# Selective attention on one core: each score row split into the larger and the smaller of its two halves before the largest values are picked

## The chip, the cores and the metric

The kernel runs on one core of one Trainium2 chip. The metric is the device time in microseconds (us) of one execution of the whole program. The engines named here are PE (TensorE, matrix products), DVE (VectorE), ACT (ScalarE), POOL (GpSimd) and SP (SyncE, which issues transfers). They run side by side and wait for each other on semaphores.

## The reference, cut to what matters

The program is a chain of four blocks over 4 sequences of 512 tokens with 128 channels. The change lies in the attention of the third block: 16 heads of 8 channels, and for every query only the largest scores take part.

```python
NHEAD = 16
FACTOR = 5
U = min(L, int(FACTOR * math.log(L)) if L > 1 else L)      # 31 for L = 512
scores = jnp.einsum('bhqd,bhkd->bhqk', Q, K) / math.sqrt(D)
thresh = jax.lax.top_k(scores, U)[0][..., -1:]
scores = jnp.where(scores < thresh, -jnp.inf, scores)
attn = jax.nn.softmax(scores, axis=-1)
context = jnp.einsum('bhqk,bhkd->bhqd', attn, V)
```

So for each of 4 x 16 x 512 score rows of 512 values the 31st largest must be found, and smaller ones drop out of the softmax.

## The kernel before, in words

`full_attention` serves two attentions of the program: this one (`top` is true) and a smaller one in the fourth block, with 8 heads and no selection. The work is cut into tiles of 128 queries by 512 keys of one head, one score row to a partition. Four heads make a quad, two neighbouring tiles of a quad a pair. The selective attention has 64 quads and 128 pairs; `p` counts pairs.

Each engine has a program of its own, written out as a loop over `p`, and the semaphores set the order. For a pair:

- PE multiplies queries and keys of a quad (`score`, L1636), and ACT copies the products from PSUM to one of eight score buffers in SBUF (`copy_scores`, L1723), three pairs ahead.
- DVE finds the largest values (`pick`). MAX8 (L1786) writes the eight largest of a row in order; the replacement (L1788), which runs as MATCH_VALUE_LOAD and MATCH_REPLACE8, copies the row with these eight overwritten by a very low value. Four rounds of MAX8 with three replacements between them give 32 values in order. The two rows of a pair take turns, so that each instruction waits for the last but one. At the end DVE waits for all picks and writes the negated and scaled maximum of both rows (TENSOR_SCALAR of 2 columns, L1792).
- ACT waits for the negated maximum and takes the exponential (`exponential`, L1707).
- POOL waits for it too. For each of the two rows it compares the scores with the 31st largest (TENSOR_SCALAR, L1812, output `kept`) and multiplies the exponentials by the result (TENSOR_TENSOR, L1815).
- PE transposes the products (`turn`, L1645), ACT copies them (L1714), PE multiplies by the values (`weigh`, L1655).

Every four quads, that is every eight pairs, a step is finished: DVE takes a reciprocal (`invert`, L1760), three pairs later multiplies by it (`normalise`, L1766), and two pairs after that adds a bias (`finish`, L1771). In DVE's loop these stand ahead of `pick` of their pair:

```python
for p in range(LAST):
    if (s := step_at(p, 3)) is not None:
        invert(s)
    if (s := step_at(p, 6)) is not None:
        normalise(s)
    if (s := step_at(p, 8)) is not None:
        finish(s)
    if p < 2 * Q:
        pick(p)
```

Elsewhere in the program, `add_product` adds a gated result to the residual: POOL multiplies four slices (L242) and DVE adds each when it is there (L248). A stage of the second block multiplies by decays on DVE (L1382) and on POOL (L1411), and an earlier line of that stage multiplies on DVE (L1364) while POOL clears a buffer (MEMSET, L1400).

Of the kernel before, what the change touches and what calls it, by code (L numbers as in the profile page):

```python
# [17 lines left out]
P = 128  # L18
# [232 lines left out]
class Memory:  # L251


    def __init__(self, nc, ctx):
        self.nc = nc
        self.slabs = ctx.enter_context(nc.sbuf_tensor("slabs", [P, NSLAB * TOK], F32))
        where, width = offsets(CONST_PARTS)
        self.const = ctx.enter_context(nc.sbuf_tensor("constants", [P, width], F32))
        self.psum = ctx.enter_context(nc.psum_tensor("psum", [P, 8, 512], F32))
        self.masks = ctx.enter_context(nc.sbuf_tensor("window_masks", [P, 320], F32))[:, :]  # L260
        self.weights = ctx.enter_context(nc.sbuf_tensor("weights", [P, 5632], F32))

        def constant(name, rows=P):
            at, n = where[name]
            return self.const[0:rows, at:at + n]

        self.mean, self.ident = constant("mean"), constant("ident")
        self.centre, self.mean_halves = constant("centre"), constant("mean_halves")
        self.tiny, self.ones_row = constant("tiny"), constant("ones_row", 1)
# [1251 lines left out]
A_PARTS = [("q2", 4 * P), ("k2", 4 * P), ("v2", P), ("o2", 4 * P), ("v_row2", P), ("bq2", 4), ("bk2", 4), ("bo2", 1), ("pick2", 4)]  # L1521


def attention_plan(selective):


    if selective:
        quads = [[(b, t, 4 * c + i, i) for i in range(4)] for b in range(BATCH) for t in range(4) for c in range(4)]
    else:
        quads = []  # L1530
        for b in range(BATCH):
            quads += [[(b, 0, i, i) for i in range(4)], [(b, 0, 4 + i, i) for i in range(4)], [(b, 1, i, i) for i in range(4)],
                      [(b, 2, 0, 0), (b, 2, 1, 1), (b, 3, 0, 2)]]
    return quads


def full_attention(nc, m, xn, out, w, heads, scale, top, key_slab, query_slab, mask=None):
# [6 lines left out]
    dh, groups = P // heads, heads // 4  # L1544
    width = dh + 1
    quads = attention_plan(top)
    Q, STEPS, passes = len(quads), len(quads) // 4, 7 if top else 1
    present = sum(len(quad) for quad in quads[0:4])
    keys = m.slab(key_slab, groups).rearrange("p (g t) -> p g t", g=groups)
    q = m.slab(query_slab, groups).rearrange("p (g t) -> p g t", g=groups)  # L1550
# [1 line left out]
    scores = [m.slab(13 + n // 4)[:, 512 * (n % 4):512 * (n % 4) + 512] for n in range(8)]  # L1552
    probs = [m.slab(15)[:, 512 * n:512 * n + 512] for n in range(4)]
    probsT = [m.slab(16 + n // 4)[:, 512 * (n % 4):512 * (n % 4) + 512].rearrange("p (k q) -> p k q", k=4) for n in range(8)]
    work = [m.slab(18)[:, 512 * n:512 * n + 512] for n in range(2)]
    kept = [m.slab(18)[:, 1024 + 512 * n:1536 + 512 * n] for n in range(2)]
    ctx = m.slab(19)[:, 0:512].rearrange("p (c q) -> p c q", c=4)
    normed = m.slab(19)[:, 512:1024].rearrange("p (c q) -> p c q", c=4)
# [56 lines left out]

    with phase(nc, "score_product scores_copied picked0 picked1 picked2 picked3 negmax_ready exp_done kept_ready probs_ready "
                   "pT_product pT_copied pv_done ctx_copied den_product inverted expanded spread_product normed_ready "
                   "out_product out_done") as (
            block, score_product, scores_copied, picked0, picked1, picked2, picked3, negmax_ready, exp_done, kept_ready, probs_ready,
            pT_product, pT_copied, pv_done, ctx_copied, den_product, inverted, expanded, spread_product, normed_ready,  # L1620
            out_product, out_done):
        finished = probs_ready if top else exp_done
        LAST = 2 * Q + 12

# [126 lines left out]
        @block.vector  # L1751
        def _(dve):
            picked = [picked0, picked1, picked2, picked3]
            taken = [0, 0, 0, 0]

            def invert(s):
                dve.wait_ge(den_product, s + 1)
                if s >= 1:
                    dve.wait_ge(expanded, s)
                nc.vector.reciprocal(inverse, ps[:, 7, 0:present]).then_inc(inverted, 1)  # L1760

            def normalise(s):
                dve.wait_ge(spread_product, s + 1)
                if s >= 1:
                    dve.wait_ge(out_product, s)
                nc.vector.tensor_tensor(normed, ctx, ps[:, 7, :].rearrange("p (c q) -> p c q", c=4), ALU.mult).then_inc(normed_ready, 1)  # L1766

            def finish(s):
                dve.wait_ge(out_product, s + 1)
                if top:  # L1770
                    nc.vector.tensor_scalar(out[:, s * P:s * P + P], ps[:, 7, 0:P], w["bo"], None, ALU.add).then_inc(out_done, 1)  # L1771
                else:
                    nc.vector.scalar_tensor_tensor(out=out[:, cols(s)], in0=ps[:, 7, :], scalar=w["bo"], in1=mask,
                                                   op0=ALU.add, op1=ALU.mult).then_inc(out_done, 1)

            def pick(p):
                own = pair(p)
                b, slot = quads[own[0][0]][0][0], 4 * (own[0][0] % 2) + own[0][1]
                dve.wait_ge(scores_copied, number(*own[-1]) + 1)
                for k in range(passes):  # L1780
                    for side in range(len(own)):
                        eight = tops[:, slot + side, 8 * (k // 2):8 * (k // 2) + 8]
                        if k:
                            dve.wait_ge(picked[b], taken[b] - len(own) + 1)
                        if k % 2 == 0:
                            nc.vector.max(eight, work[side] if k else scores[slot + side]).then_inc(picked[b], 1)  # L1786
                        else:
                            nc.vector.match_replace(out=work[side], in_to_replace=eight, in_values=scores[slot + side] if k == 1 else work[side],  # L1788
                                                    imm_value=MASKED).then_inc(picked[b], 1)
                        taken[b] += 1  # L1790
                dve.wait_ge(picked[b], taken[b])
                nc.vector.tensor_scalar(tops[:, slot:slot + len(own), 32], tops[:, slot:slot + len(own), 0], -scale, None,  # L1792
                                        ALU.mult).then_inc(negmax_ready, 1)

            for p in range(LAST):
                if (s := step_at(p, 3)) is not None:
# [3 lines that stand above are left out]
                if (s := step_at(p, 8)) is not None:  # L1800
                    finish(s)
                if p < 2 * Q:
                    pick(p)

        if top:
            @block.gpsimd
            def _(pool):
                for p in range(2 * Q):
                    for g, j in pair(p):
                        n, slot = number(g, j), 4 * (g % 2) + j  # L1810
                        pool.wait_ge(negmax_ready, p + 1)
                        nc.gpsimd.tensor_scalar(kept[n % 2], scores[slot], tops[:, slot, TOPK - 1:TOPK], None, ALU.is_ge).then_inc(kept_ready, 1)  # L1812
                        pool.wait_ge(kept_ready, n + 1)
                        pool.wait_ge(exp_done, n + 1)
                        nc.gpsimd.tensor_tensor(probs[j], probs[j], kept[n % 2], ALU.mult).then_inc(probs_ready, 1)  # L1815
# [827 lines left out]
```

## Time and profile before

| | us |
|---|---|
| median of 3 runs | 5038.49 |
| the three runs | 5038.49, 5037.72, 5050.88 |
| span of the profiled execution | 5048.7 |
| DVE busy in it | 3273.2 |
| PE busy | 3797.4 |
| ACT busy | 2549.2 |
| POOL busy | 2087.9 |

The span runs from the first to the last instruction of the profiled execution; the list of runs doesn't mark which of the three it is. Busy times are sums over stages that have different limits, so the stage of the change is looked at by itself. An instruction's recorded time reaches from its start to its end, and on DVE the next may start before that end; what an instruction costs its engine is the distance from its start to the next start.

### The profile page before, as it was taken

Reading aid. Unit: us, or ns where it says so; the run is one execution under the profiler, and the core shown is the slowest. Engines: PE = TensorE matmul, PEld = TensorE weight load, DVE = VectorE, ACT = ScalarE, POOL = GpSimd, SP = SyncE. Lnnn points to the kernel's source line nnn. Section 1 sums busy time; section 2 is a strip of 40 time slices with the busy share of each in tenths; the row PEclk is TensorE's granted clock in tenths of the full one; section 3 lists DMA queues with packets and bytes.
Section 4 is the critical chain, followed back from the end, with each engine's and each line's share of the span. In section 5 each row is a group of like instructions: output and inputs, shape, how many; then the busy total and the mean of one; then the engine's idle time right before and its main releaser. Section 6 shows DMA issues by size and latency. Waiting matters only on the chain. (4 is left out here: it accounts for less than half of the span.)

```text
span 5048.7 us, 81560 instructions
## 1 busy us (share of the span) xinstructions
PE 3797.4 (75%) x28548; PEld 2346.0 (46%) x28548; DVE 3273.2 (65%) x6732; ACT 2549.2 (50%) x7024; POOL 2087.9 (41%) x1599
## 2 busy tenths in 40 slices
PE   5288788788789788797778659766666666587897
PEld 2156466466466465564253533333333333355664
DVE  5777476476575575674352643599999999832344
ACT  2199498498597695794121211233333333335443
POOL 0177276375474573671222200266666666500000
PEclk8599899899899899998586878755555555567998
DMA  0011111111111111111000000000000000000000
GB/s 18 28 43 47 36 47 46 36 49 47 36 46 52 30 47 51 34 47 48 0 1 9 1 26 0 0 1 1 1 1 1 1 1 1 1 7 11 12 1 9
DMA packets 48662, 110.09 MB, mean 22 GB/s; under 512 B 8944, under 2 KB 9200, under 8 KB 46704
## 3 DMA queue, kind: packets, MB, share of 16 engines
q1 hardware_dynamic: 48240, 104.66, 6.7%
q8 instruction: 241, 3.95, 0.3%
q14 instruction: 181, 1.48, 0.1%
HBM read 31.23 MB, written 1.05 MB: 6 GB/s over the span
## 5 line engine op out<-in xcount | busy, mean ns | idle before, releaser
L1089 POOL TENSOR_TENSOR slabs<-slabs 128x512 f32<-128x512 f32 x768 | 953.2, 1274 | 379.7 <-DVE slabs L956 322.5
L1786 DVE MAX8 slabs<-slabs 128x8 f32<-128x512 f32 x1084 | 695.1, 686 | 58.3 <-ACT slabs L1723 58.3
L1812 POOL TENSOR_SCALAR slabs<-slabs 128x512 f32<-128x512 f32 x256 | 400.2, 1563 | 470.4 <-DVE slabs L1792 470.4
L1707 ACT ACTIVATE slabs<-slabs 128x512 f32<-128x512 f32 x316 | 212.1, 721 | 727.5 <-DVE slabs L1792 727.5
L859 ACT ACTIVATE slabs<-slabs 128x96 f32<-128x96 f32 x1536 | 556.5, 366 | 19.2 <-PE psum L670 13.3
L1645 PE MATMUL psum<-constants,slabs 128*128 128x128 f32 x1264 | 306.3, 407 | 299.2 <-POOL slabs L1815 298.9
L1788 DVE MATCH_REPLACE8 slabs<-slabs 128x512 f32<-128x512 f32 x768 | 515.5, 683 | 0.0
L623 PE MATMUL psum<-slabs 128*128 128x512 f32 x768 | 411.7, 663 | 128.5 <-DVE slabs L956 63.0
L1078 POOL TENSOR_TENSOR slabs<-slabs 128x768 f32<-128x768 f32 x192 | 282.3, 1470 | 499.1 <-DVE slabs L931 499.1
L1636 PE MATMUL psum<-slabs 8*128 8x512 f32 (+1 forms) x632 | 346.2, 1086 | 164.4 <-ACT slabs L1723 164.1
L1645 PEld LDWEIGHTS psum<-constants,slabs 128*128 128x128 f32 x1264 | 223.3, 209 | 383.4 <-POOL slabs L1815 343.3
L941 DVE TENSOR_REDUCE slabs<-slabs 128x16 f32<-128x1024 f32 x192 | 234.2, 1220 | 225.2 <-ACT slabs L810 225.2
L670 PE MATMUL psum<-constants,slabs 128*96 128x128 f32 x1536 | 245.0, 283 | 153.8 <-ACT slabs L852 151.2
L1815 POOL TENSOR_TENSOR slabs<-slabs 128x512 f32<-128x512 f32 x256 | 325.2, 1270 | 21.4
L623 PEld LDWEIGHTS psum<-slabs 128*128 128x128 f32 x768 | 151.4, 210 | 353.7 <-issue 186.2
L242 POOL TENSOR_TENSOR slabs<-slabs 128x512 f32<-128x512 f32 x12 | 17.5, 1486 | 665.9 <-POOLq L63 665.9
L859 ACT ACTIVATION_READ_ACCUMULATOR slabs<-slabs 128x1 f32 x1536 | 292.3, 190 | 0.0
L810 ACT ACTIVATE slabs<-psum 128x1024 f32<-128x1024 f32 x192 | 196.7, 1025 | 140.9 <-PE psum L623 131.4
L964 DVE TENSOR_TENSOR slabs<-slabs 128x512 f32<-128x512 f32 x384 | 248.7, 688 | 28.2 <-POOL slabs L1089 28.0
L1636 PEld LDWEIGHTS psum<-slabs 8*128 8x128 f32 (+1 forms) x632 | 112.6, 293 | 301.4 <-ACT slabs L1723 282.2
L852 ACT ACTIVATE slabs<-psum 96x512 f32<-96x512 f32 x384 | 222.5, 579 | 43.1 <-PE psum L670 42.9
L670 PEld LDWEIGHTS psum<-constants,slabs 128*96 128x96 f32 x1536 | 155.1, 128 | 190.5 <-issue 173.7
(389 smaller groups left out, 7979.6 us busy)
## 6 DMA issues: line engine op xcount, KB each, us to landing
slabs<-slabs SPq DMA_DIRECT2D x192, 192.0 KB, 2.5
slabs<-slabs SPq DMA_DIRECT2D x192, 128.0 KB, 2.5
slabs<-F1A SPq DMA_DIRECT2D x7, 2176.0 KB, 8.4
slabs<-slabs SPq DMA_DIRECT2D x144, 64.0 KB, 2.1
slabs<-F1F SPq DMA_DIRECT2D x6, 580.5 KB, 4.9
slabs<-S SPq DMA_DIRECT2D x4, 645.0 KB, 5.8
weights<-M SPq DMA_DIRECT2D x1, 2184.0 KB, 9.4
weights<-R SPq DMA_DIRECT2D x2, 1079.5 KB, 5.1
```

The source lines that it names most:

```text
L623: last = nc.tensor.matmul(ps[:, i, :], tokens, w(name, 512 * half, 512), start=True, stop=True)
L670: last = nc.tensor.transpose(ps[0:KEYS, 7, n * P:n * P + P], probs[:, 4 * part + n, :], m.ident)
L859: last = nc.scalar.activation(probs[:, n, :], masked[:, n, :], ACT.Exp, bias=shifts[:, n:n + 1], accum_out=denom[:, n:n + 1])
L964: nc.vector.tensor_tensor(roped[:, at, :].rearrange("p h (s i) -> p h s i", s=2), cosines[:, at, :].rearrange("p h (s i) -> p h s i", s=2) ...
L1078: nc.gpsimd.tensor_tensor(probs, probs, scale, ALU.mult).then_inc(probs_ready, 1)
L1089: nc.gpsimd.tensor_tensor(out[:, at, :], normed[u % 2][:, at, :], table, ALU.mult).then_inc(rope_done, 1)
L1636: nc.tensor.matmul(ps[:, j, :], q[rows, h // 4, b * SEQ + t * P:b * SEQ + t * P + P], keys[rows, h // 4, cols(b)], start=True, stop=True). ...
L1645: last = nc.tensor.transpose(ps[:, 4 + n % 2, k * P:k * P + P], probs[j][:, k * P:k * P + P], m.ident)
L1786: nc.vector.max(eight, work[side] if k else scores[slot + side]).then_inc(picked[b], 1)
L1788: nc.vector.match_replace(out=work[side], in_to_replace=eight, in_values=scores[slot + side] if k == 1 else work[side], imm_value=MASKED). ...
L1812: nc.gpsimd.tensor_scalar(kept[n % 2], scores[slot], tops[:, slot, TOPK - 1:TOPK], None, ALU.is_ge).then_inc(kept_ready, 1)
L1815: nc.gpsimd.tensor_tensor(probs[j], probs[j], kept[n % 2], ALU.mult).then_inc(probs_ready, 1)
```

## The change

In the selective attention `pick_top` takes the place of `pick`. It first forms, for both rows of a pair in one instruction, the minimum and the maximum of columns 0 to 255 with columns 256 to 511. It picks the 16 largest of the minima (two rounds of MAX8 with one replacement), which are written beside the 256 maxima, and then the 32 largest among these 272. The negated maximum is written after the second of the four rounds, without a wait of its own. POOL waits for the count of picks of a pair (20) in place of the negated maximum. The minima and maxima lie in a new buffer, `annex`. The attention without selection keeps `pick`, with its one round of MAX8.

```diff
@@ -259,6 +259,7 @@
         self.weights = ctx.enter_context(nc.sbuf_tensor("weights", [P, 5632], F32))
+        self.annex = ctx.enter_context(nc.sbuf_tensor("annex", [P, 2304], F32))
@@ -1521,6 +1522,10 @@
+HALVED = SEQ // 2
+LISTED = HALVED + 16
+PICKS = 20
@@ -1552,7 +1557,8 @@
-    work = [m.slab(18)[:, 512 * n:512 * n + 512] for n in range(2)]
+    leads = [m.annex[:, 2 * LISTED * n:2 * LISTED * n + 2 * LISTED].rearrange("p (s k) -> p s k", s=2) for n in range(2)]
+    trails = [m.annex[:, 4 * LISTED + SEQ * n:4 * LISTED + SEQ * n + SEQ].rearrange("p (s k) -> p s k", s=2) for n in range(2)]
@@ -1777,20 +1783,50 @@
                 dve.wait_ge(scores_copied, number(*own[-1]) + 1)
-                for k in range(passes):
-                    for side in range(len(own)):
-                        eight = tops[:, slot + side, 8 * (k // 2):8 * (k // 2) + 8]
-                        if k:
-                            dve.wait_ge(picked[b], taken[b] - len(own) + 1)
-                        if k % 2 == 0:
-                            nc.vector.max(eight, work[side] if k else scores[slot + side]).then_inc(picked[b], 1)
-                        else:
-                            nc.vector.match_replace(out=work[side], in_to_replace=eight, in_values=scores[slot + side] if k == 1 else work[side],
-                                                    imm_value=MASKED).then_inc(picked[b], 1)
-                        taken[b] += 1
+                for side in range(len(own)):
+                    nc.vector.max(tops[:, slot + side, 0:8], scores[slot + side]).then_inc(picked[b], 1)
+                taken[b] += len(own)
                 dve.wait_ge(picked[b], taken[b])
                 nc.vector.tensor_scalar(tops[:, slot:slot + len(own), 32], tops[:, slot:slot + len(own), 0], -scale, None,
                                         ALU.mult).then_inc(negmax_ready, 1)
+
+            def pick_top(p):
+                own = pair(p)
+                b, slot = quads[own[0][0]][0][0], 4 * (own[0][0] % 2) + own[0][1]
+                both = m.slab(13 + slot // 4)[:, 512 * (slot % 4):512 * (slot % 4) + 1024].rearrange("p (s h k) -> p s h k", s=2, h=2)
+                dve.wait_ge(scores_copied, number(*own[-1]) + 1)
+                lead, trail = leads[p % 2], trails[p % 2]
+                nc.vector.tensor_tensor(trail, both[:, :, 0, :], both[:, :, 1, :], ALU.min).then_inc(parted, 1)
+                nc.vector.tensor_tensor(lead[:, :, 0:HALVED], both[:, :, 0, :], both[:, :, 1, :], ALU.max).then_inc(parted, 1)
+                dve.wait_ge(parted, 2 * p + 1)
+
+                def largest(out, among):
+                    nc.vector.max(out, among).then_inc(picked[b], 1)
+                    taken[b] += 1
+
+                def strike(eight, among):
+                    dve.wait_ge(picked[b], taken[b] - 1)
+                    nc.vector.match_replace(out=among, in_to_replace=eight, in_values=among, imm_value=MASKED).then_inc(picked[b], 1)
+                    taken[b] += 1
+
+                for side in range(2):
+                    largest(lead[:, side, HALVED:HALVED + 8], trail[:, side, :])
+                for side in range(2):
+                    strike(lead[:, side, HALVED:HALVED + 8], trail[:, side, :])
+                for side in range(2):
+                    dve.wait_ge(picked[b], taken[b] - 1)
+                    largest(lead[:, side, HALVED + 8:LISTED], trail[:, side, :])
+                dve.wait_ge(parted, 2 * p + 2)
+                for k in range(4):
+                    for side in range(2):
+                        dve.wait_ge(picked[b], taken[b] - 1)
+                        largest(tops[:, slot + side, 8 * k:8 * k + 8], lead[:, side, :])
+                    if k == 1:
+                        nc.vector.tensor_scalar(tops[:, slot:slot + 2, 32], tops[:, slot:slot + 2, 0], -scale, None,
+                                                ALU.mult).then_inc(negmax_ready, 1)
+                    if k < 3:
+                        for side in range(2):
+                            strike(tops[:, slot + side, 8 * k:8 * k + 8], lead[:, side, :])
@@ -1800,7 +1836,7 @@
                 if p < 2 * Q:
-                    pick(p)
+                    (pick_top if top else pick)(p)
@@ -1808,7 +1844,7 @@
-                        pool.wait_ge(negmax_ready, p + 1)
+                        pool.wait_ge([picked0, picked1, picked2, picked3][quads[g][0][0]], PICKS * (p % (Q // 2) + 1))
```

The diff also adds the semaphore `parted` and drops the name `passes`.

## Rows read from the trace of the kernel before

**Rows 1.** Groups by line, 3480 to 4280 us: count | busy, mean ns | idle

```profile
L1786 DVE MAX8 slabs<-slabs 128x8 f32<-128x512 f32 x708 | 453.9, 686 | 0.0
```

**Rows 2.** Busy time by stretch: length, PE, PEld, DVE, ACT, POOL, clock, DMA

```profile
3480.00:4280.00 800.00, 492.34 (x2691) 283.33 (x2692) 796.98 (x1894) 297.86 (x554) 500.88 (x356) 0.56 0.00 1
```

**Rows 3.** POOL's line L1812: duration min/median/max ns, first and last start

```profile
L1812 POOL TENSOR_SCALAR slabs<-slabs x256: 1554/1563/1574, 3236.0 to 4385.2; 128x512 f32<-128x512 f32 x128
```

**Rows 4.** Timeline of DVE, one pair: start, us, engine, line, operation

```profile
3803.76 0.17 DVE L1792 TENSOR_SCALAR slabs<-slabs 128x2 f32<-128x2 f32 x1
3803.84 1.28 DVE L1786 MAX8 slabs<-slabs 128x8 f32<-128x512 f32 x2
3805.03 0.08 DVE L1788 MATCH_VALUE_LOAD slabs<-slabs 128x8 f32 x1
3805.09 0.68 DVE L1788 MATCH_REPLACE8 slabs<-slabs 128x512 f32<-128x512 f32 x1
3805.69 0.09 DVE L1788 MATCH_VALUE_LOAD slabs<-slabs 128x8 f32 x1
...
3812.68 0.17 DVE L1792 TENSOR_SCALAR slabs<-slabs 128x2 f32<-128x2 f32 x1
```

**Rows 5.** Timeline of POOL, the same pair

```profile
3804.03 1.56 POOL L1812 TENSOR_SCALAR slabs<-slabs 128x512 f32<-128x512 f32 x1 [3.71 <-DVE slabs L1792]
3805.68 1.27 POOL L1815 TENSOR_TENSOR slabs<-slabs 128x512 f32<-128x512 f32 x1
3806.93 1.56 POOL L1812 TENSOR_SCALAR slabs<-slabs 128x512 f32<-128x512 f32 x1
```

**Rows 6.** Timeline of the residual sum, POOL and DVE

```profile
2961.27 1.26 POOL L242 TENSOR_TENSOR slabs<-slabs 128x512 f32<-128x512 f32 x1
2961.35 1.73 DVE L248 TENSOR_TENSOR slabs<-slabs 128x512 f32<-128x512 f32 x1 [2.23 <-POOL slabs L242]
2962.49 1.71 POOL L242 TENSOR_TENSOR slabs<-slabs 128x512 f32<-128x512 f32 x1
2963.00 1.75 DVE L248 TENSOR_TENSOR slabs<-slabs 128x512 f32<-128x512 f32 x1
...
2966.34 0.68 DVE L248 TENSOR_TENSOR slabs<-slabs 128x512 f32<-128x512 f32 x1
```

**Rows 7.** Timeline of the decay products, two places, POOL and DVE

```profile
2537.27 0.74 POOL L1411 TENSOR_TENSOR slabs<-slabs 128x256 f32<-128x256 f32 x1 [1.35 <-PE psum L1328]
2537.31 0.98 DVE L1382 TENSOR_TENSOR slabs<-slabs 128x256 f32<-128x256 f32 x1
...
2544.50 0.96 POOL L1411 TENSOR_TENSOR slabs<-slabs 128x256 f32<-128x256 f32 x1 [1.40 <-PE psum L1328]
2544.51 0.41 DVE L1382 TENSOR_TENSOR slabs<-slabs 128x256 f32<-128x256 f32 x1
...
2544.84 1.30 DVE L1376 COPY_PREDICATED slabs<-weights,psum 128x1024 f32<-128x1024 int32 x1
```

**Rows 8.** Timeline, DVE beside a MEMSET of POOL

```profile
2522.93 1.22 DVE L1364 TENSOR_TENSOR slabs<-slabs 128x1024 f32<-128x1024 f32 x1 [1.18 <-PEq L63]
2523.18 1.80 POOL L1400 MEMSET slabs<- 128x2048 f32 x1 [30.54 <-SPq L58]
```

**Rows 9.** Timeline around a reciprocal and around a bias sum

```profile
3333.80 0.25 DVE L1760 RECIPROCAL slabs<-psum 128x16 f32<-128x16 f32 x1
...
3333.97 0.64 DVE L1786 MAX8 slabs<-slabs 128x8 f32<-128x512 f32 x1
3333.99 1.56 POOL L1812 TENSOR_SCALAR slabs<-slabs 128x512 f32<-128x512 f32 x1 [3.11 <-DVE slabs L1792]
...
3379.06 0.35 DVE L1771 TENSOR_SCALAR slabs<-psum,slabs 128x128 f32<-128x128 f32 x1
...
3379.25 1.56 POOL L1812 TENSOR_SCALAR slabs<-slabs 128x512 f32<-128x512 f32 x1 [3.10 <-DVE slabs L1792]
3379.32 0.69 DVE L1786 MAX8 slabs<-slabs 128x8 f32<-128x512 f32 x1
```

More of the change, by code:

```diff
@@ L1546, in full_attention @@
     quads = attention_plan(top)
-    Q, STEPS, passes = len(quads), len(quads) // 4, 7 if top else 1
+    Q, STEPS = len(quads), len(quads) // 4
     present = sum(len(quad) for quad in quads[0:4])
@@ L1617, in full_attention @@
                    "pT_product pT_copied pv_done ctx_copied den_product inverted expanded spread_product normed_ready "
-                   "out_product out_done") as (
+                   "out_product out_done parted") as (
             block, score_product, scores_copied, picked0, picked1, picked2, picked3, negmax_ready, exp_done, kept_ready, probs_ready,
             pT_product, pT_copied, pv_done, ctx_copied, den_product, inverted, expanded, spread_product, normed_ready,
-            out_product, out_done):
+            out_product, out_done, parted):
         finished = probs_ready if top else exp_done
```

## The prediction

> **What bounds the kernel now.** I read the busy shares by stretch first, then the lines of one stretch, then the timeline of one pair, and last the places elsewhere in the trace where VectorE and GpSimd run two-input instructions side by side, because the change brings such instructions into this stage.
>
> The stage is the selective attention. In 800 us of its middle VectorE is busy for 797.0 us, PE for 492.3, GpSimd for 500.9 and ACT for 297.9 [rows 2]. So VectorE sets the pace, and every other engine has room. GpSimd's first instruction of a pair comes 128 times, from 3236.0 to 4385.2 us [rows 3]: there are 128 pairs of score rows, one each 9.0 us (the last pair has two of them, some 2.9 us apart [rows 5], so 1146.3 us over 127 pairs).
>
> A MAX8 over 512 columns is recorded with 686 ns [rows 1], but such instructions overlap: two of them take 1.19 us from the first start to what follows, so one costs 0.595 us of VectorE; a MATCH_VALUE_LOAD costs 0.06, and the replacement behind it 0.60 [rows 4]. From one negated maximum to the next are 8.92 us [rows 4]. The parts are eight MAX8 (4.76) and six loads with replacements (6 x 0.66 = 3.96), together 8.72, and the TENSOR_SCALAR (0.08 to the next start); the 0.12 left is its wait for the last MAX8 to end. That TENSOR_SCALAR ends at 3803.93 [rows 4]; GpSimd, which waits for it, starts at 3804.03, 0.10 later, and needs 1.56 + 1.27 us for each of two rows [rows 5], 5.7 us in all, of the 8.9.
>
> **The price of a column.** A TENSOR_TENSOR over 256 columns that nobody held up took 0.33 us to the next start (2544.51 to 2544.84) [rows 7]; one instruction over 512 columns takes 0.595 [rows 4]. That is 0.265 us for 256 columns and 0.065 us a piece for being an instruction at all. For MAX8 and the replacement at 256 and 272 columns no row stands; from the two lengths I take 0.33 and 0.345 us. The ends come from instructions with almost no columns: the load of 8 columns costs 0.06 and the TENSOR_SCALAR of 2 columns 0.08 [rows 4], so the fixed part lies between 0.05 and 0.08, and a piece is at most 0.015 us cheaper or dearer.
>
> **The change, part by part.** Per pair it removes eight MAX8 and six replacements over 512 columns and the wait ahead of the TENSOR_SCALAR: 8.92 us. It adds
>
> - the minimum and the maximum of the halves, two TENSOR_TENSOR of 2 x 256 columns: 2 x 0.595 = 1.19
> - on the smaller halves four MAX8 (4 x 0.33 = 1.32) and two loads with replacements (2 x 0.39 = 0.78)
> - on the 272 candidates eight MAX8 (8 x 0.345 = 2.76) and six loads with replacements (6 x 0.405 = 2.43)
> - the negated maximum, now in mid-pair and with nothing to wait for: 0.08.
>
> That is 8.56 if nothing holds VectorE up: 0.36 us less for a pair, 46 us over 128 pairs, far less than the fewer columns promise, since 14 long instructions become 22. Each wait inside still has one instruction of the other row in between, 0.33 us or more, and a piece runs some 0.09 us beyond its slot (0.69 against 0.595), so the waits cost nothing: I count them so, with 0.05 us a pair as their upper end.
>
> The negated maximum comes earlier by some 3 us, and with it ACT's exponential; that is nothing, since ACT has 500 of 800 us free. GpSimd no longer waits for the negated maximum but for the 20th pick, which is the last MAX8 of the pair: it starts where it started, and loses only the 0.17 us of the TENSOR_SCALAR. One more semaphore and the smaller attention, which keeps its own path, are counted at nothing.
>
> **What the two new TENSOR_TENSOR meet.** They read two SBUF tensors each, and they stand at the head of a pair, just where GpSimd begins on the pair before. The trace has this meeting in the residual sums. GpSimd's TENSOR_TENSOR, 1.26 us alone, ran from 2961.27 to 2962.53. VectorE's, issued at 2961.35 (0.68 us when alone), ended at 2963.08, 0.55 us after GpSimd's end: it was not slowed but stood until GpSimd was done. GpSimd's next, issued at 2962.49, took 1.71 us, 0.45 longer, as if started at 2962.94, 0.14 before VectorE's end. VectorE's next, issued at 2963.00, was again 0.55 us behind GpSimd's end at 2964.20 [rows 6]. They take turns in the order of asking, each holding the other off for a whole instruction, and of two VectorE instructions in a row the second does not get in ahead of a waiting GpSimd. In the decay products VectorE came first when it was issued 0.01 us after GpSimd and came second when it was 0.04 after [rows 7].
>
> The Trainium skill has this as a rule ("SBUF — State Buffer", section "Who interferes with whom"): a VectorE instruction with two SBUF inputs and a GpSimd instruction that reads SBUF exclude each other for a whole instruction. The rows on the residual sums agree, 1.73 us for 0.68; by the rule GpSimd's compare holds VectorE off just as its product does, which gives the likeliest sum below.
>
> What no row shows is whether GpSimd's TENSOR_SCALAR (one SBUF tensor and a number per row) holds VectorE off as its TENSOR_TENSOR does. One end is the whole 1.56 us; the other is nothing, as with GpSimd's MEMSET, beside which a VectorE TENSOR_TENSOR of 1024 columns took 1.22 us and so lost nothing [rows 8] (0.68 and another 512 columns, 0.53, make 1.21). MEMSET reads nothing, TENSOR_SCALAR reads as many columns as a product has in one operand: it is nearer to TENSOR_TENSOR, and I take the whole.
>
> Now one pair, with 0 at the issue of the minimum. The last MAX8 before it was issued at -0.345 and ends at +0.09; GpSimd's compare is issued 0.10 later, at 0.19. The minimum has been first by 0.19 and ends at 0.69. The compare starts in effect 0.14 before that, at 0.55, and ends at 2.11. The maximum was issued at 0.60, behind the compare: it ends 0.55 after it, at 2.66, and the next VectorE instruction starts 0.08 earlier (2963.00 against 2963.08), at 2.58. Undisturbed it would be 1.19: **1.39 us of standing for each of 127 pairs, 177 us.**
>
> In three of eight pairs an instruction of the finishing steps stands ahead of the minimum. The bias sum delays it by 0.26 us; GpSimd is issued 0.07 before that (3379.25 against 3379.32) [rows 9] and so comes first. Then the compare ends at 1.75, the minimum at 2.30; the product, asked for at 1.84, ends at 2.16 + 1.27 = 3.43, the maximum at 3.98, the next starts at 3.90 where 1.45 was due: 2.45 us, 1.06 more than in a plain pair. Behind the normalising product, 512 columns and so 0.60, it is the same 3.90 against 1.79: 2.11, 0.72 more. Behind the reciprocal the minimum is issued 0.02 us before GpSimd (3333.97 against 3333.99) [rows 9] and I count it as a plain pair; if it comes second, 15 pairs cost 1.1 us more, 17 us. With 14 bias sums and 15 normalisings inside the loop this adds 15 + 11 = 26 us.
>
> GpSimd's own chain grows by 0.36 us for the compare and by 0.32 for the first product, which waits for the maximum (asked for at 2.20, in effect started at 2.52); it ends at 6.7, and the negated maximum is due at 2.58 + 2.10 + 0.69 + 0.81 + 0.69 = 6.87, just behind. So that instruction meets nothing, GpSimd doesn't become the bound and has nothing left running when the next minimum comes.
>
> **Sum:** -46 + 177 + 26 = **+157 us**. On the profiled execution, 5048.7 us of span, that is 5206. The list of times doesn't say which of its three is the profiled one; the largest, 5050.88, lies 2.2 us over the span. Against the median of 5038.49, 10.2 below the span, the forecast is **5196 us**, slower by 3.1%. About 0.3%, 15 us, is what a measurement of this kernel can tell from no change.
>
> **Rivals.**
>
> *The standing does not happen (faster).* GpSimd's compare doesn't hold the second read, as MEMSET doesn't, or the maximum follows the minimum without GpSimd coming between. Then 5038.5 - 46 = 4992. For it: no row has a TENSOR_SCALAR on GpSimd against a two-input VectorE instruction. Against it: both residual pairs of instructions in rows took turns [rows 6]. It decides from below 0.36 us of standing per pair on. Chance 0.14.
>
> *The negated maximum stands instead.* If the compare doesn't block, GpSimd's second product runs from 4.75 to 6.02 while the negated maximum is due at 5.48. Should even so small a VectorE TENSOR_SCALAR exclude GpSimd, it stands for 0.54 us per pair, 69 us, and the time is 5038.5 - 46 + 69 = 5061; with half of that, about 5027, which counts as no change. The Trainium skill's same section names tensor_scalar among the instructions that can hold the pair; no run here shows it at two columns. Chance 0.05 within 0.3%, and 0.05 for partial holding that ends between 5054 and 5150.
>
> *Both stand in every pair.* If the compare gets in before the minimum, every pair stands for 3.90 - 1.19 = 2.71 us: 127 x 2.71 = 344, and 5038.5 - 46 + 344 = 5337. The 0.19 us of lead speak against it, since 0.01 behind was enough to come first [rows 7]. Chance 0.06.
>
> **How the numbers follow.** The likeliest, 0.70, gives 5196; its own range is 5154 to 5261 (the two ends of the fixed part, 22 instructions by 0.015 by 128, are 42 us each way; above, the reciprocal adds 17 and the waits 6). The whole range must hold 0.8: with partial holding and no change it goes from 5025 to 5260 and leaves out the faster case and the doubled one, 0.2. Faster 0.14, same 0.05, slower 0.81.
>
> **What the new profile would show.** The minimum with about 0.69 us in most pairs and the maximum with about 2.06; both near 2 us in two of eight pairs; GpSimd's compare at about 1.9 for the first row of a pair and 1.56 for the second, the first product at about 1.6; MAX8 at 0.42 to 0.44; plain pairs 9.95 us apart, and some 1306 us from GpSimd's first compare to its last, 1149 now; VectorE still without idle gaps, since a standing instruction counts as busy. The prediction is wrong if the maximum shows 0.69 us, or if pairs are nearer than 8.9.

## The result

The changed kernel took 5005.06 us (median of 4 runs, 5000.08 to 5008.33) beside 5038.27 for the kernel before: ratio 0.9928, 95% interval 0.9913 to 0.9942. It is faster by 33 us, where 157 us more were forecast. Its profiled execution spans 4998.3 us. One of the eight runs with the negated maximum at the end of a pair, further down, was a slow one (6901.89 us, granted clock 0.761 against 0.793 to 0.797) and is left out of its median.

The groups by line of the changed kernel, 3480 to 4280 us (columns as in [rows 1]):

```profile
L1848 POOL TENSOR_SCALAR slabs<-slabs 128x512 f32<-128x512 f32 x183 | 356.7, 1949 | 199.7 <-DVE slabs L1804 199.7
L1804 DVE MAX8 slabs<-annex 128x8 f32<-128x272 f32 x728 | 280.5, 425 | 0.0
...
L1804 DVE MAX8 annex<-annex 128x8 f32<-128x256 f32 x364 | 134.7, 409 | 0.0
...
L1800 DVE TENSOR_TENSOR annex<-slabs 128x512 f32<-128x512 f32 x91 | 66.8, 734 | 0.0
L1799 DVE TENSOR_TENSOR annex<-slabs 128x512 f32<-128x512 f32 x91 | 62.3, 685 | 0.0
```

The minimum (L1799) has 0.685 us and the maximum (L1800) 0.734, so VectorE hardly stands; GpSimd's compare (L1848) rose from 1.56 to 1.95 us in the mean. The two engines still hold each other up, but GpSimd pays for it, and GpSimd has time to spare. VectorE is busy all 800 us of the stretch, GpSimd 585:

```profile
3480.00:4280.00 800.00, 472.08 (x2794) 280.71 (x2792) 800.00 (x2854) 313.36 (x568) 585.15 (x365) 0.54 0.00 1
```

A plain pair in the timeline of the changed kernel, VectorE and GpSimd (answers to [rows 4, 5]; ACT and PE left out):

```profile
3800.92 0.67 DVE L1799 TENSOR_TENSOR annex<-slabs 128x512 f32<-128x512 f32 x1
...
3801.10 2.52 POOL L1848 TENSOR_SCALAR slabs<-slabs 128x512 f32<-128x512 f32 x1 [1.81 <-DVE slabs L1804]
3801.51 0.68 DVE L1800 TENSOR_TENSOR annex<-slabs 128x512 f32<-128x512 f32 x1
3802.11 0.75 DVE L1804 MAX8 annex<-annex 128x8 f32<-128x256 f32 x2
...
3804.95 1.56 POOL L1848 TENSOR_SCALAR slabs<-slabs 128x512 f32<-128x512 f32 x1
...
3806.41 0.15 DVE L1825 TENSOR_SCALAR slabs<-slabs 128x2 f32<-128x2 f32 x1
...
3806.60 1.27 POOL L1851 TENSOR_TENSOR slabs<-slabs 128x512 f32<-128x512 f32 x1
```

GpSimd's compare is issued 0.18 us behind the minimum, as forecast, and should have got in before the maximum. It did not: it takes 2.52 us, 0.96 more than alone, and so starts in effect at 3802.06, 0.13 before the maximum's end: it waits for both VectorE instructions. 83 of the 127 pairs are like this one. The second compare of the pair, with VectorE at one-input work, has its 1.56. Behind a reciprocal (15 pairs) the compare is issued 0.02 us behind the minimum and waits for both as well (2.55 us).

Around a bias sum (L1777) it goes another way:

```profile
3782.86 0.33 DVE L1777 TENSOR_SCALAR slabs<-psum,slabs 128x128 f32<-128x128 f32 x1
3783.04 2.10 POOL L1848 TENSOR_SCALAR slabs<-slabs 128x512 f32<-128x512 f32 x1 [1.81 <-DVE slabs L1804]
3783.11 0.67 DVE L1799 TENSOR_TENSOR annex<-slabs 128x512 f32<-128x512 f32 x1
3783.71 1.09 DVE L1800 TENSOR_TENSOR annex<-slabs 128x512 f32<-128x512 f32 x1
...
3788.11 1.27 POOL L1851 TENSOR_TENSOR slabs<-slabs 128x512 f32<-128x512 f32 x1
...
3789.02 0.38 DVE L1825 TENSOR_SCALAR slabs<-slabs 128x2 f32<-128x2 f32 x1
```

Here the compare is issued 0.07 us ahead of the minimum. The minimum is still first, but the maximum stands (1.09 for 0.68). Later in that pair the negated maximum of 2 columns takes 0.38 us and ends at 3789.40, just behind GpSimd's product (3789.38): so small an instruction stands too. Behind the normalising product (L1772) the minimum stands a little:

```profile
3765.15 1.56 POOL L1848 TENSOR_SCALAR slabs<-slabs 128x512 f32<-128x512 f32 x1 [1.80 <-DVE slabs L1804]
3765.55 0.83 DVE L1799 TENSOR_TENSOR annex<-slabs 128x512 f32<-128x512 f32 x1
3766.31 0.68 DVE L1800 TENSOR_TENSOR annex<-slabs 128x512 f32<-128x512 f32 x1
```

It was issued 0.40 us behind the compare, and the maximum followed 0.16 late (0.76 against 0.60), so the compare kept it off only until about 0.56 us after the compare's start, though that ran for 1.56.

From one negated maximum to the next is 8.58 us (median; 8.91 before). 128 x 0.34 is 43 us gained. The pairs with a bias sum lose 0.41 at the maximum and 0.24 at the negated maximum, 14 times, those with a normalising product 0.15, 15 times: 11 us. That leaves 32, the measured gain.

### The profile page after: what moved, and what is told of

It reads as the page before. It is cut to its first block and busy times, and to the rows that moved or that the text cites. A ratio compares the mean times of both kernels' runs of the same rounds, so it can differ in the third digit from the quotient of the medians.

```text
span 4998.3 us, 82970 instructions
## 1 busy us (share of the span) xinstructions
PE 3727.4 (75%) x28548; PEld 2323.5 (46%) x28548; DVE 3243.7 (65%) x8012; ACT 2552.9 (51%) x7024; POOL 2185.2 (44%) x1599
## 5 line engine op out<-in xcount | busy, mean ns | idle before, releaser
L1651 PE MATMUL psum<-constants,slabs 128*128 128x128 f32 x1264 | 327.4, 416 | 470.5 <-POOL slabs L1851 469.9
L1848 POOL TENSOR_SCALAR slabs<-slabs 128x512 f32<-128x512 f32 x256 | 501.7, 1960 | 335.8 <-DVE slabs L1804 335.8
L1804 DVE MAX8 slabs<-annex 128x8 f32<-128x272 f32 x1024 | 394.4, 424 | 0.0
L1809 DVE MATCH_REPLACE8 annex<-slabs,annex 128x272 f32<-128x272 f32 x768 | 319.4, 421 | 0.0
L1642 PE MATMUL psum<-slabs 8*128 8x512 f32 (+1 forms) x632 | 273.6, 1089 | 16.7 <-ACT slabs L1729 16.6
L1720 ACT ACTIVATE slabs<-psum 128x512 f32<-128x512 f32 x316 | 181.0, 588 | 118.5 <-PE psum L1651 118.5
```

The lines of the kernel that those rows point to most:

```text
L1642: nc.tensor.matmul(ps[:, j, :], q[rows, h // 4, b * SEQ + t * P:b * SEQ + t * P + P], keys[rows, h // 4, cols(b)], start=True, stop=True). ...
L1651: last = nc.tensor.transpose(ps[:, 4 + n % 2, k * P:k * P + P], probs[j][:, k * P:k * P + P], m.ident)
L1804: nc.vector.max(out, among).then_inc(picked[b], 1)
L1809: nc.vector.match_replace(out=among, in_to_replace=eight, in_values=among, imm_value=MASKED).then_inc(picked[b], 1)
```

## The experiments

Diffs are against the changed kernel unless another is named. The first four runs share their runs of the kernel before (5041.0 us), the next three theirs (5043.04), the last three theirs (5039.12).

**The changed kernel again**, without an edit.

> The changed kernel once more, beside the experiments. 5005 us, 33 below the kernel before: pairs of 8.57 us and a mean of 8.77 with the finishing steps. Theory and rival expect the same here; it is the mark for the others.

4997.38 us, ratio 0.9911 (0.9896 to 0.9925); negated maxima again 8.58 us apart.

**The finishing steps behind the negated maximum.**

```diff
                     if k == 1:
                         nc.vector.tensor_scalar(tops[:, slot:slot + 2, 32], tops[:, slot:slot + 2, 0], -scale, None,
                                                 ALU.mult).then_inc(negmax_ready, 1)
+                        steps(p)
...
-                if (s := step_at(p, 3)) is not None:
-                    invert(s)
-                if (s := step_at(p, 6)) is not None:
-                    normalise(s)
-                if (s := step_at(p, 8)) is not None:
-                    finish(s)
```

`steps` holds the six lines taken out. The smaller attention still runs them at the head of a pair.

> In the selective attention the three finishing steps of VectorE move from the head of a pair to behind the negated maximum. Theory (what stands on VectorE depends on whether GpSimd's compare was issued before the minimum, which the finishing steps bring about): every pair now looks like a plain one, maximum 0.68 us, no stretched minimum, no negated maximum of 0.38; per step 0.15 + 0.41 + 0.25 us go, times 15 about 11 us, so 4994. Rival (the finishing steps cost what they cost wherever they stand): no change from the changed kernel, 5005.

4991.35 us, ratio 0.9903 (0.9889 to 0.9917). No minimum or maximum stands any more (minimum, maximum, duration min/median/max in ns):

```profile
L1807 DVE TENSOR_TENSOR annex<-slabs x128: 660/672/718, 3211.6 to 4315.4; 128x512 f32<-128x512 f32 x128
L1808 DVE TENSOR_TENSOR annex<-slabs x128: 671/683/731, 3212.2 to 4315.9; 128x512 f32<-128x512 f32 x128
```

The mean distance of the negated maxima fell from 8.77 to 8.69 us, 127 x 0.08 = 10 us, where the theory says 11. The two medians differ by 6 us and their intervals overlap, so by total time alone this version is not told apart from the changed kernel; it has the lowest median of all and is below the kernel before.

**The negated maximum back at the end of a pair.**

```diff
-                    if k == 1:
+                    if k == 3:
+                        dve.wait_ge(picked[b], taken[b])
                         nc.vector.tensor_scalar(tops[:, slot:slot + 2, 32], tops[:, slot:slot + 2, 0], -scale, None,
                                                 ALU.mult).then_inc(negmax_ready, 1)
```

> The negated maximum goes back to the end of a pair, with its wait. Alone that costs 0.12 us of waiting a pair, 15 us, less some 3 us for the 14 negated maxima that met GpSimd's product: 5017. But it also puts the minimum 0.12 us behind the last MAX8's end, with GpSimd's compare issued 0.10 behind it, that is 0.02 before the minimum. Theory (a compare issued ahead gets its columns between minimum and maximum, as behind the bias sum): the maximum shows 1.1 us in most pairs and 128 x 0.41 = 52 us come on top, 5070. Rival (the two VectorE instructions go through together whenever the lead is this small): 5017 and a maximum of 0.68.

5058.13 us (median of seven), ratio 1.0035 (1.0024 to 1.0046): this one order takes more than the whole gain. The timeline of one of its pairs:

```profile
3789.37 2.06 POOL L1849 TENSOR_SCALAR slabs<-slabs 128x512 f32<-128x512 f32 x1 [2.84 <-DVE slabs L1804]
3789.38 0.71 DVE L1799 TENSOR_TENSOR annex<-slabs 128x512 f32<-128x512 f32 x1
3790.01 1.09 DVE L1800 TENSOR_TENSOR annex<-slabs 128x512 f32<-128x512 f32 x1
```

A compare issued 0.01 us ahead of the minimum gets in before the maximum, one issued 0.18 behind does not. The theory's 1.1 us shows in the 83 plain pairs, which are 9.15 us apart. In the 44 pairs with a finishing step the compare comes 0.2 to 0.6 us ahead of the minimum, and the maximum has its 0.68.

**The negated maximum moved, the rows whole.** Against the kernel before:

```diff
                         taken[b] += 1
-                dve.wait_ge(picked[b], taken[b])
-                nc.vector.tensor_scalar(tops[:, slot:slot + len(own), 32], tops[:, slot:slot + len(own), 0], -scale, None,
-                                        ALU.mult).then_inc(negmax_ready, 1)
+                    if k == min(2, passes - 1):
+                        if passes == 1:
+                            dve.wait_ge(picked[b], taken[b])
+                        nc.vector.tensor_scalar(tops[:, slot:slot + len(own), 32], tops[:, slot:slot + len(own), 0], -scale, None,
+                                                ALU.mult).then_inc(negmax_ready, 1)
...
-                        pool.wait_ge(negmax_ready, p + 1)
+                        pool.wait_ge([picked0, picked1, picked2, picked3][quads[g][0][0]], 14 * (p % (Q // 2) + 1))
```

> The kernel before with one part of the change alone: the negated maximum behind the second round, GpSimd waiting for the count of picks; the rows stay whole, 512 columns. Theory (the halving itself is worth 0.2 us a pair, the moved negated maximum 0.12 to 0.2): a pair falls from 8.92 to 8.76, 128 x 0.16 = 20 us, so about 5018. Rival (the wait ahead of the negated maximum was worth nothing, all of the gain is the halving): 5038.

5026.18 us, ratio 0.9966 (0.9954 to 0.9979), 15 us of the 20 forecast; pairs are 8.78 us apart (median of the distances, as above). So the moved negated maximum gives 0.13 us of a pair's 0.34 and the halving 0.20. The rival falls.

**The compare without its number per row.**

```diff
-nc.gpsimd.tensor_scalar(kept[n % 2], scores[slot], tops[:, slot, TOPK - 1:TOPK], None, ALU.is_ge).then_inc(kept_ready, 1)
+nc.gpsimd.tensor_scalar(kept[n % 2], scores[slot], 0.0, None, ALU.is_ge).then_inc(kept_ready, 1)
```

> GpSimd's compare takes a constant, 0.0, in place of the 31st largest of each row, so it reads one tensor and no number per row; the selection is left out and the output differs. Theory (the compare asks for the second read twice, first for its number per row and some 0.15 us later for its columns; in a plain pair the minimum holds up the first ask, so that the maximum is ahead of the second): with the columns as the only ask it gets in between minimum and maximum in every plain pair, the maximum shows 1.0 to 1.1 us in place of 0.68, the compare about 1.9 to 2.0 in place of 2.52, and 113 plain pairs lose 0.4 us each, 45 us: about 5045. Rival (two VectorE instructions without a wait between them keep the second read once the first has it): maximum 0.68, compare 2.5, 5000 as the changed kernel.

4996.88 us, ratio 0.9913 (0.9897 to 0.993). The theory of two asks fell:

```profile
3329.17 0.81 DVE L1799 TENSOR_TENSOR annex<-slabs 128x512 f32<-128x512 f32 x1
3329.48 2.45 POOL L1848 TENSOR_SCALAR slabs<-slabs 128x512 f32<-128x512 f32 x1 [1.96 <-DVE slabs L1804]
3329.76 0.82 DVE L1800 TENSOR_TENSOR annex<-slabs 128x512 f32<-128x512 f32 x1
```

The records of both are longer, but the starts (0.59 apart) and so the pair are not: VectorE does not stand. The compare still waits for both, and so does the longest one, behind a bias sum and issued 0.05 us ahead of the minimum (duration min/median/max in ns):

```profile
L1848 POOL TENSOR_SCALAR slabs<-slabs x256: 1477/1490/2714, 3226.5 to 4334.6; 128x512 f32<-128x512 f32 x128
```

That holds in 13 of the 14 pairs with a bias sum; in the other one the compare, 0.067 us ahead, went first. Behind a reciprocal it waited for both in 13 of 15 and got in between in two. VectorE's records begin up to 0.14 us early in this run: in every plain pair the compare is issued 0.50 us before the minimum's end, while the minimum's length goes from 0.67 to 0.81. Counted from that end the compare behind a bias sum comes where it came in the changed kernel, some 0.75 us before, and there it got in ahead of the maximum.

**Two tensors in place of the compare.**

```diff
-nc.gpsimd.tensor_scalar(kept[n % 2], scores[slot], tops[:, slot, TOPK - 1:TOPK], None, ALU.is_ge).then_inc(kept_ready, 1)
+nc.gpsimd.tensor_tensor(kept[n % 2], scores[slot], scores[slot], ALU.mult).then_inc(kept_ready, 1)
```

> GpSimd's compare becomes a TENSOR_TENSOR that multiplies the score row by itself, two tensors of 512 columns; the selection is left out and the output differs. Theory (a GpSimd instruction that asks for its columns at once takes its turn after the minimum, and one with two tensors holds the second read to its end, as in rows 6 of the kernel before): the maximum shows about 1.8 us, the first GpSimd instruction of a pair 1.7, a plain pair takes 8.57 + 1.1 = 9.7 us, and 127 x 1.1 = 140 us come on top of the changed kernel: about 5140. Rival (two VectorE instructions without a wait between them keep the second read): maximum 0.68, the GpSimd instruction about 2.2, time about 5000.

5076.92 us, ratio 1.0066 (1.0049 to 1.0082). Both sides missed the time. In the plain pairs the rival was right; maximum and GpSimd's first instruction:

```profile
L1800 DVE TENSOR_TENSOR annex<-slabs x128: 678/695/1752, 3225.3 to 4410.3; 128x512 f32<-128x512 f32 x128
...
L1848 POOL TENSOR_TENSOR slabs<-slabs x256: 1032/1048/2016, 3233.5 to 4421.9; 128x512 f32<-128x512 f32 x128
```

The median maximum has 0.695 us, and GpSimd waits, 2.01 us in place of 1.04. What costs are the negated maxima, which stand for 0.26 us in the plain pairs, GpSimd's work being shorter, and the pairs with a finishing step, where the maximum shows 1.52 to 1.75. Around a reciprocal:

```profile
3330.53 0.63 DVE L1799 TENSOR_TENSOR annex<-slabs 128x512 f32<-128x512 f32 x1
3330.54 1.51 POOL L1848 TENSOR_TENSOR slabs<-slabs 128x512 f32<-128x512 f32 x1 [3.12 <-DVE slabs L1804]
3331.08 1.52 DVE L1800 TENSOR_TENSOR annex<-slabs 128x512 f32<-128x512 f32 x1
```

Issued with the minimum, 0.01 us behind, GpSimd takes the turn that it doesn't get at 0.16 behind.

**Work between minimum and maximum.**

```diff
-                nc.vector.tensor_tensor(lead[:, :, 0:HALVED], both[:, :, 0, :], both[:, :, 1, :], ALU.max).then_inc(parted, 1)
...
                 for side in range(2):
                     largest(lead[:, side, HALVED:HALVED + 8], trail[:, side, :])
+                nc.vector.tensor_tensor(lead[:, :, 0:HALVED], both[:, :, 0, :], both[:, :, 1, :], ALU.max).then_inc(parted, 1)
```

> The maximum moves behind the first two MAX8 over the minima, so that 0.66 us of VectorE work without a second SBUF input lies between minimum and maximum. Theory (the compare reads its number and then its columns while VectorE leaves the second read free, and lets go before the maximum): compare about 2.0 us in place of 2.52 in plain pairs, maximum 0.68 there and behind the bias sum too (0.41 gained, 14 times, 6 us); behind the normalising product the maximum now meets GpSimd's product, which has two tensors and holds the second read to its end, and stands for about 1 us, 15 times, 15 us: about 5008, not to be told from the changed kernel by its time. Rival (what the compare loses is not the second read but a fixed cost of running beside VectorE's TENSOR_TENSOR): compare still 2.5.

5093.93 us, ratio 1.0101 (1.0084 to 1.0117), 86 us above the forecast for it. The first two rows below are as the theory has them, the compare at 1.92 and the maximum free. The time went into the last one:

```profile
3311.72 1.92 POOL L1848 TENSOR_SCALAR slabs<-slabs 128x512 f32<-128x512 f32 x1 [3.14 <-DVE slabs L1803]
...
3312.92 0.67 DVE L1813 TENSOR_TENSOR annex<-slabs 128x512 f32<-128x512 f32 x1
...
3316.61 1.26 POOL L1851 TENSOR_TENSOR slabs<-slabs 128x512 f32<-128x512 f32 x1
...
3317.14 0.76 DVE L1825 TENSOR_SCALAR slabs<-slabs 128x2 f32<-128x2 f32 x1
```

A shorter compare brings GpSimd's second product 0.6 us forward, and the negated maximum now meets it in 112 of 127 pairs: 0.76 us for 0.15, until the product ends at 3317.87. That is some 0.6 us a pair, 67 us; another 0.11 us a pair, 14 us, is VectorE's wait for the minimum's end. In the changed kernel the negated maximum ends just ahead of that product (3806.56 against 3806.60), since the first compare is held up.

**Three in a row.**

```diff
                 nc.vector.tensor_tensor(lead[:, :, 0:HALVED], both[:, :, 0, :], both[:, :, 1, :], ALU.max).then_inc(parted, 1)
-                dve.wait_ge(parted, 2 * p + 1)
+                spare = m.slab(18)[:, 0:SEQ].rearrange("p (s k) -> p s k", s=2)
+                nc.vector.tensor_tensor(spare, both[:, :, 0, :], both[:, :, 1, :], ALU.max).then_inc(parted, 1)
+                dve.wait_ge(parted, 3 * p + 1)
...
-                dve.wait_ge(parted, 2 * p + 2)
+                dve.wait_ge(parted, 3 * p + 3)
```

> A third TENSOR_TENSOR of the same halves, its result unused, stands directly behind the maximum. Theory (turns go by the order of asking, and a VectorE instruction that waits for nothing asks while the one ahead of it is still reading: the maximum asks before GpSimd's compare, the third one after it): the compare stays near 2.5 us, the third instruction stands for about 0.4 us (1.1 us in the record), and the negated maximum, pushed to 6.5 us, meets GpSimd's second product for 0.4 us: 127 x (0.6 + 0.4 + 0.4) = 178 us, about 5180. Rival (VectorE keeps the second read as long as its next two-input instruction waits for nothing): third instruction 0.68 us, compare 3.1 us, 128 x 0.6 = 76 us, about 5080.

5107.89 us, ratio 1.0135 (1.0118 to 1.0152). The rival was right on the mechanism in the 83 plain pairs, which are 9.18 us apart, 0.60 more:

```profile
3808.60 0.67 DVE L1799 TENSOR_TENSOR annex<-slabs 128x512 f32<-128x512 f32 x1
3808.78 3.12 POOL L1850 TENSOR_SCALAR slabs<-slabs 128x512 f32<-128x512 f32 x1 [1.80 <-DVE slabs L1806]
3809.19 0.68 DVE L1800 TENSOR_TENSOR annex<-slabs 128x512 f32<-128x512 f32 x1
3809.79 0.68 DVE L1802 TENSOR_TENSOR slabs<-slabs 128x512 f32<-128x512 f32 x1
```

The some 30 us over its forecast are in two kinds of pairs where GpSimd does get in ahead of the third. Behind a normalising product (15 pairs, some 16 us) the minimum had stood for 0.15 us:

```profile
3819.11 0.68 DVE L1800 TENSOR_TENSOR annex<-slabs 128x512 f32<-128x512 f32 x1
3819.60 1.31 POOL L1853 TENSOR_TENSOR slabs<-slabs 128x512 f32<-128x512 f32 x1
3819.71 1.75 DVE L1802 TENSOR_TENSOR slabs<-slabs 128x512 f32<-128x512 f32 x1
```

Behind a reciprocal (15 pairs, some 10 us with the negated maximum) nothing had stood. The compare, issued 0.02 us behind the minimum, lets two go by and not the third, in all 15:

```profile
3559.79 0.62 DVE L1799 TENSOR_TENSOR annex<-slabs 128x512 f32<-128x512 f32 x1
3559.81 2.54 POOL L1850 TENSOR_SCALAR slabs<-slabs 128x512 f32<-128x512 f32 x1 [1.79 <-DVE slabs L1806]
...
3560.93 1.09 DVE L1802 TENSOR_TENSOR slabs<-slabs 128x512 f32<-128x512 f32 x1
```

**A wait between them.**

```diff
-                nc.vector.tensor_tensor(lead[:, :, 0:HALVED], both[:, :, 0, :], both[:, :, 1, :], ALU.max).then_inc(parted, 1)
                 dve.wait_ge(parted, 2 * p + 1)
+                nc.vector.tensor_tensor(lead[:, :, 0:HALVED], both[:, :, 0, :], both[:, :, 1, :], ALU.max).then_inc(parted, 1)
```

> The maximum waits for the minimum to end, a wait without other purpose. Theory and rival of the run before both expect that the compare now gets in between, as GpSimd did in rows 6 of the kernel before, where each addition waited for its product: compare about 1.95 us, maximum about 1.0, 0.14 + 0.24 us more for VectorE in a plain pair, and GpSimd's second product, now 0.6 us sooner, meets the negated maximum for about 0.5 us: 127 x 0.9 = 110 us, about 5115. If the compare still shows 2.5 us, the wait is not what decides and both fall.

5081.57 us, ratio 1.0082 (1.0065 to 1.0098). The wait decides:

```profile
3801.23 0.67 DVE L1799 TENSOR_TENSOR annex<-slabs 128x512 f32<-128x512 f32 x1
3801.41 1.92 POOL L1848 TENSOR_SCALAR slabs<-slabs 128x512 f32<-128x512 f32 x1 [3.14 <-DVE slabs L1804]
3801.94 1.07 DVE L1801 TENSOR_TENSOR annex<-slabs 128x512 f32<-128x512 f32 x1
```

Pairs are 9.30 us apart, 0.73 more where 0.9 were expected, since the negated maximum stands for 0.23 us and not 0.5. This wait holds VectorE up: the maximum starts 0.04 us behind the minimum's end (3801.23 + 0.67), where it started 0.08 ahead of it. Whether the wait counts or the gap is not told apart.

**Work between them, the negated maximum sooner.** Against the kernel with the work between:

```diff
-                    if k == 1:
-                        nc.vector.tensor_scalar(tops[:, slot:slot + 2, 32], tops[:, slot:slot + 2, 0], -scale, None,
-                                                ALU.mult).then_inc(negmax_ready, 1)
...
                             strike(tops[:, slot + side, 8 * k:8 * k + 8], lead[:, side, :])
+                            if k == 0 and side == 0:
+                                dve.wait_ge(picked[b], taken[b] - 1)
+                                nc.vector.tensor_scalar(tops[:, slot:slot + 2, 32], tops[:, slot:slot + 2, 0], -scale, None,
+                                                        ALU.mult).then_inc(negmax_ready, 1)
```

> The kernel with the maximum moved behind two MAX8, and the negated maximum moved as well, from behind the second round to the middle of the first three (behind the first replacement on the 272), where GpSimd is in the second half of its second compare. Theory (the 97 us that moving the maximum cost are the negated maximum of 2 columns, 0.76 us in place of 0.15, standing until GpSimd's second product ends): negated maximum 0.15 us, and the time falls from 5094 to about 5015 (0.11 us of waiting after the minimum and the maxima behind the normalising product stay). Rival (it is the place of the maximum itself that costs): 5094 as before.

5062.77 us, ratio 1.0047 (1.003 to 1.0063): 31 of the 97 us came back, not 79. The place of the negated maximum does move the time, but the place I chose was not free:

```profile
3813.17 1.56 POOL L1849 TENSOR_SCALAR slabs<-slabs 128x512 f32<-128x512 f32 x1
...
3814.25 0.51 DVE L1829 TENSOR_SCALAR slabs<-slabs 128x2 f32<-128x2 f32 x1
```

Issued 1.08 us after the compare, it ends at 3814.76, just behind the compare's end at 3814.73, and the replacement behind it takes 0.70 us for 0.43. A minimum was let go 0.56 us after the compare's start.

## Why the prediction was wrong

**What held.** VectorE bounds the stage. The price of a pair without standing was 8.56 us, measured 8.58: MAX8 starts are 0.33 us apart at 256 columns and 0.34 to 0.35 at 272, so halving the columns does not halve the price (0.595 us at 512), and with 22 long instructions for 14 the halving leaves 0.20 us a pair. The 46 us that this was to gain were 43. In a plain pair the compare is issued 0.17 to 0.19 us behind the minimum (0.19 forecast), and VectorE's TENSOR_TENSOR and GpSimd's instructions do exclude each other. Both signs of being wrong that the prediction names came: the maximum shows 0.68 us in plain pairs, and these are 8.58 us apart.

**The step that failed** is the order: "of two VectorE instructions in a row the second does not get in ahead of a waiting GpSimd". In a plain pair it does. So in place of 1.39 us of standing on VectorE, 177 us in all, GpSimd waits 0.96 us a pair, of some 2.8 that it had to spare (1.81 of them still idle). "The read" stands in what follows for what the two engines cannot have at once; the runs show that they exclude each other, not what they share.

The rows on the residual sums had two conditions that the new pair of instructions has not: each addition has a wait ahead of it, and the first had itself stood behind GpSimd. A wait that holds VectorE up brings GpSimd in between by itself (the run with the waiting maximum). In the residual sums, though, the second addition's product had ended 0.47 us before it started (at 2962.53) [rows 6], so its wait was over, and which of the two conditions decided there stays open. With neither condition VectorE keeps the read, in plain pairs, through two instructions and through three. Having stood goes with GpSimd's turn behind the normalising product (three in a row, 1.75 us); that it is the cause is inferred from such places, not tried by itself. A GpSimd instruction issued ahead of the minimum or with it (0.01 us) also gets the next turn. Two things don't fit these conditions and stay open: the compare with a constant, which waited for both even when issued 0.05 ahead (2.71 us), and the compare behind a reciprocal, issued 0.02 behind, which waits for two of two and for only two of three.

The rival "the standing does not happen", at 4992 and 0.14, was the outcome, 13 us from the first measurement; its second clause, the maximum following the minimum without GpSimd between, was the reason. Its first clause was not: GpSimd's compare does hold VectorE off, by 0.41 us behind a bias sum.

**A second step was mis-sized** and would have mattered: the compare does not hold the read for its whole 1.56 us but for about 0.56 from its start. Where GpSimd does get in between, the maximum stands 0.41 us and not 1.39. The kernel with the negated maximum at the end, where that happens in the 83 plain pairs, took 5058 us, not 5196, and some 15 us of it (127 x 0.12, an estimate) are its wait. The Trainium skill ("SBUF — State Buffer", "SBUF: two separate sides") says that of a VectorE instruction with two SBUF inputs and a GpSimd instruction that reads SBUF, the one that starts first has the ports that the two share for the whole instruction. The trace agrees for GpSimd's TENSOR_TENSOR [rows 6] and for the 2-column TENSOR_SCALAR, which stood to the compare's very end, and not for a TENSOR_TENSOR behind the compare (0.56 of 1.56).

**The bias sum and the normalising product** were forecast at 2.45 and 2.11 us of standing; they show 0.41 + 0.24 and 0.15: the minimum is first behind a bias sum though issued 0.07 us later than the compare, and the hold was taken too long. The reciprocal was rightly counted as a plain pair.

**The negated maximum** of 2 columns does exclude GpSimd. The rival that says so had the right mechanism in the wrong pairs: in plain ones it is issued 5.49 us behind the minimum, 0.10 before the second compare's end and 0.19 before the product.

## What to carry to other kernels

When two engines exclude each other, ask who pays: in the plain pairs here a VectorE run of two-input instructions without a wait between them made GpSimd wait for all of it, which cost nothing since GpSimd had time to spare, and a single wait between them, or a GpSimd instruction that comes just ahead of the run, hands the bill to VectorE (0.4 us a pair; with the negated maximum and its wait at the end of a pair 4997 became 5058 us). Before taking over a rule of turns from other rows, compare the waits around the instructions, and what each had just waited for, as well as the instructions. Changing when GpSimd starts also moves everything later that excludes it, down to an instruction of 2 columns (0.15 to 0.76 us).

## What the runs showed of the hardware that was not expected

- GpSimd's TENSOR_SCALAR keeps a VectorE TENSOR_TENSOR off for some 0.56 us of its 1.56, but a VectorE TENSOR_SCALAR of 2 columns until its end (0.51 us, ending 0.03 behind it).
- VectorE held GpSimd off through three TENSOR_TENSOR in a row: 3.12 us for a compare of 1.56. Issued 0.02 us behind the first of them and not 0.18, the compare came in ahead of the third (2.54 us).
